# Feed-forward stage of a decoder layer: maxima and projection at other places, weights with semaphores of their own, side taps of the last blocks on ScalarE and GpSimd

## The chip, the cores and the metric

One core of a Trainium2 chip runs the whole layer. The metric is device time in microseconds (us), as the median of the runs of the kernel.

## What is computed

The layer takes x (4 sequences of 1024 tokens, 512 features) and a context, and computes linear attention, then cross attention with an S4D convolution and a feed-forward part, then a convolutional feed-forward with quantised weights and activations; each is followed by a residual and a layer normalisation. Only the last two pieces matter here. Cut to them:

```
h  = layernorm(xt, g_ffn, b_ffn)
xt = xt + gelu(h @ W1 + b1) @ W2 + b2          # 512 -> 2048 -> 512
x2 = layernorm(x1 + layernorm(xt, g_out, b_out))

h = bit_linear(x2, w1)                          # tokens x 2048
h = silu(depthwise_conv1d(h, conv_w, 3 taps) + conv_b)
out = layernorm(x2 + bit_linear(h, w2))
# bit_linear: activations rounded to 8 bits by their row's largest
# absolute value, weights to -1, 0, 1 by their mean absolute value
```

## The kernel before, in words

The change lies in `feed_forward`, the last stage (L1644 on). Each engine has a program of its own, written out by hand in the order in which it runs; semaphores join them. All five programs step through slots `t` = 0 to 38. Slot t does for token tile t (128 tokens, 32 tiles) the products with W1 (`up`, L1868, 16 groups of 128 channels) and with W2 (`down`, L1876). Its layer normalisations are spread over slots t-1 to t+1: `tail_a` to `tail_d` on VectorE (DVE), the square roots (`root`) on ScalarE (ACT), `finish` on GpSimd (POOL). `store_q` writes the rounded tile to memory two slots later.

The convolutional part works on blocks n of 256 tokens, with n = t // 2 - 2. Half of a block's 16 channel tiles is done in an even slot, half in the odd one: `spread` (the product with w1, four matmuls between the groups of `down`, L1887), `dequantise` (DVE, L2117), `centre` (the middle tap, ACT, L1974), `first_tap` and `last_tap` (DVE, L2123 and L2129), `silu` (ACT, L1982). In the next even slot `largest` (DVE, L2159) takes the maxima over the channels, `turn_max` (TensorE, PE, L1895) transposes them, `scales` (DVE) makes the row scales, `spread_scale` (PE, L1900) copies them to all partitions, and `requantise` (DVE, L2179) rounds. In the odd slot after that `project` (PE, L1906, twice 16 matmuls) does the product with w2, `copy_y` (ACT, L1987) empties it, `add_rest` (POOL) adds the residual.

What holds each step, beside its inputs: `up` has 8 places in PSUM and may begin group 8 only when ACT's `gelu` has emptied groups 0 to 3. ACT takes `root(1, t-1)` ahead of `gelu`, and that needs DVE's `tail_a(t-1)`, behind `largest`. The two halves of `project` share one PSUM bank, so the second one waits for `copy_y` of the first. A block's first `spread` waits for the block's inputs, which SP loads (`load_block`, L1800 to L1806) when the last tile of the block's halo has been stored; in three blocks of four that tile is t-2, stored by POOL in the same slot, behind `finish(t-1)`. Blocks 14 and 15 run in slots 32 to 35, in which no tile is left.

At the stage's start SP issues seven small loads, then W1 (4 MB), the next tile and W2 (4 MB); one semaphore, `ff_in`, counts all nine, and every engine waits for all nine.

```
                    if post and not odd:
                        if f == 2:
                            turn_max(n - 1)
                        if f == 9:
                            spread_scale(n - 1)
                    if post and odd and f in (5, 11):
                        project(n - 1, f // 8)
```

Of the kernel before, what the change touches and what calls it, by code (L numbers as in the profile page):

```python
# [1643 lines left out]
def feed_forward(nc, x1, ys, mod_out, W1, b1T, W2, b2, g_ffn, b_ffn, g_out, b_out, eye, x2, q1T, inv_rows,  # L1644
# [6 lines left out]
    with ExitStack() as ctx:  # L1651
# [65 lines left out]
        p_m, p_b = p_mb[:, 0, :].rearrange("p (u n) -> p u n", u=2), p_mb[:, 1, :]  # L1717
        p_y = m.ps("p_y", [P, D])

        (ff_in, consts, h_ready, hT_done, hT_copied, g_done, g_copied, o_done, mod_done, step, pstep, qb_ready, qT_done,  # L1720
         qT_copied, x2_ready, r3_ready, ln_head, out_norm, inv_done) = [m.sem(n) for n in (
             "ff_in consts h_ready hT_done hT_copied g_done g_copied o_done mod_done step pstep qb_ready qT_done "
             "qT_copied x2_ready r3_ready ln_head out_norm inv_done").split()]
        (small_in, tot_ready, sum_done, wm_ready, part_ready, v_ready, c_done, hs_ready, c1_ready, conv_step, c3_ready,
         sl_ready, half_ready, mx_ready, mt_done, dg_ready, b_done, sq_ready, q2_ready, y_done, y_copied, res_ready,
# [34 lines left out]
        def halo(n):  # L1760

            k = n % PB
            return (1 if k == 0 else 0), (WB + 1 if k == PB - 1 else WB + 2)

        block = ctx.enter_context(nc.Block())

        @block.sync
        def _(sp):
# [47 lines left out]
            for n, ap in enumerate((g_ffn, b_ffn, b2, g_out, b_out)):  # L1816
                sp.dma_start(bc[:, n, :], bcast(ap)).then_inc(ff_in, 16)
            sp.dma_start(b1c[:], b1T).then_inc(ff_in, 16)
            sp.dma_start(w1[:], W1.rearrange("(k p) n -> p k n", p=P)).then_inc(ff_in, 16)
            load_tile(1)  # L1820
            load_mod(1)
            sp.dma_start(w2[:], W2.rearrange("(k p) n -> p k n", p=P)).then_inc(ff_in, 16)
            sp.dma_start(cw[:], conv_w).then_inc(small_in, 16)
            sp.dma_start(cb[:], conv_b).then_inc(small_in, 16)
            load_piece(0)
# [19 lines left out]
        def _(pe):  # L1845
# [15 lines left out]

            def up(t, f):
                if f == 0:
                    pe.wait_ge(hT_copied, t + 1)
                if f % 4 == 0:
                    at_least(pe, g_copied, t * FT + f - 4)
                for k in range(KD):
                    last = mm(p_g[:, f % 8, :], w1[:, k, f * P:(f + 1) * P], hT[:, k * P:(k + 1) * P],  # L1868
                              start=(k == 0 and f % 4 == 0), stop=(k == KD - 1 and f % 4 == 3), skip_group_check=True)
                last.then_inc(g_done, 1)  # L1870

            def down(t, f):
                if f == 0:
                    at_least(pe, var[1], t)
                pe.wait_ge(g_copied, t * FT + f + 1)
                last = mm(p_o[:], gT[:, f, :], w2[:, f, :], start=(f == 0), stop=(f == FT - 1))  # L1876
                if f == FT - 1:
                    last.then_inc(o_done, 1)
# [27 lines left out]
                    last = mm(p_y[:], q2[:, f, u * P:(u + 1) * P], v2[:, f, :], start=(f == 0), stop=(f == FT - 1))  # L1906
                last.then_inc(y_done, 1)

            pe.wait_ge(ff_in, 16 * 9)
            pe.wait_ge(consts, 3)  # L1910
            turn_h(0)
            for t in range(SLOTS):
                n, odd = blk(t), t % 2
                ff, bit, post = tile_slot(t), is_blk(n), is_blk(n - 1)
                for f in range(FT):
                    if ff:
                        up(t, f)
                    if f == 3 and tile_slot(t - 2):
                        turn_q(t - 2)
                    if post and not odd:  # L1920
                        if f == 2:
                            turn_max(n - 1)
                        if f == 9:
                            spread_scale(n - 1)
                    if post and odd and f in (5, 11):
                        project(n - 1, f // 8)
                if t == 2:
                    pe.wait_ge(tot_ready, 1)
                    mm(p_b[:, 0:2], ones[:], tot[:], start=True, stop=True).then_inc(sum_done, 1)
                if n == 0 and not odd:  # L1930
                    pe.wait_ge(v_ready, PIECES)
                for f in range(FT):
                    if ff:
                        down(t, f)
                    if bit and not odd and f >= HF:
                        spread(n, f - HF)
                    if bit and odd and f % 2 == 0:
                        spread(n, HF + f // 2)
                    if f == 11 and tile_slot(t + 1):
                        turn_h(t + 1)  # L1940

        @block.scalar
        def _(act):
# [26 lines left out]
            def centre(n, f):  # L1970
                j = n * FT + f
                at_least(act, sl_ready, j - NBUF + 1)
                act.wait_ge(hs_ready, j + 1)
                a(c[:, f % NBUF, :], hs[:, f % NBUF, 1:WB + 1], ACT.Identity, bias=cb[:, f:f + 1],  # L1974
                  scale=cw[:, f, 1:2]).then_inc(c1_ready, 1)

# [11 lines left out]

            act.wait_ge(consts, 3)
            root(0, 0)  # L1990
            act.wait_ge(ff_in, 16 * 9)
            copy_h(0)
            for t in range(SLOTS):
                n, odd = blk(t), t % 2
# [5 lines left out]
                for f in range(FT):  # L2000
                    if ff:
                        gelu(t, f)
                    if f == 7:
                        if post and odd:
                            copy_y(n - 1, 0)
                        if tile_slot(t - 2):
                            copy_q(t - 2)
                    if f == (7 if odd else 11):
                        if tile_slot(t - 1):
                            root(2, t - 1)  # L2010
                        if tile_slot(t + 1):
                            root(0, t + 1)
# [18 lines left out]
        def _(dve):  # L2031
            v = nc.vector
            v.memset(eps[:], LN_EPS).then_inc(consts, 1)
            v.memset(ones[:], 1.0).then_inc(consts, 1)
            dve.wait_ge(ff_in, 16 * 9)
            v.tensor_copy(identb[:], ident[:]).then_inc(consts, 1)
            st = Steps(dve, step, 0)

# [74 lines left out]
            def dequantise(n, f):  # L2113
                j, (lo, hi) = n * FT + f, halo(n)
                at_least(dve, c3_ready, j - NBUF + 1)
                dve.wait_ge(c_done, j + 1)
                v.tensor_tensor(hs[:, f % NBUF, lo:hi], p_c[:, f % 2, lo:hi], rs[:, n % 2, lo:hi], ALU.mult).then_inc(hs_ready, 1)  # L2117

# [13 lines left out]
            def channels(n, half, quarter):  # L2132

                f0 = HF * half
                if quarter == 0:
# [6 lines left out]
                            st.link(v.memset(hs[:, :, WB + 1:WB + 2], 0.0))  # L2142
                    dequantise(n, f0)
                    dequantise(n, f0 + 1)
                for f in range(f0 + HF // 2 * quarter, f0 + HF // 2 * quarter + HF // 2):
                    first_tap(n, f)
                    if f + 2 < f0 + HF:
                        dequantise(n, f + 2)
                    if f > f0:
                        last_tap(n, f - 1)  # L2150
# [50 lines left out]
            for t in range(SLOTS):  # L2201
# [22 lines left out]
                    close_b(n - 2)  # L2224
                if after:
                    head_b(t + 1)
                if before and odd:
                    tail_d(t - 1)
                if t < 2:
                    for i in range(4 * t, 4 * t + 4):  # L2230
# [7 lines left out]
                        quantise(i)  # L2238
                if bit:
                    channels(n, odd, 0)  # L2240
                if before and not odd:
                    tail_d(t - 1)
                if bit:
                    channels(n, odd, 1)
# [3 lines left out]
        @block.gpsimd  # L2248
        def _(pool):
            tt = pool.tensor_tensor  # L2250
            pool.wait_ge(ff_in, 16 * 9)
            st = Steps(pool, pstep, 0)

            def modulate(t):
# [29 lines left out]
            def add_rest(n, u):  # L2284
                pool.wait_ge(y_copied, 2 * n + u + 1)
                pool.wait_ge(b_in[n % 2], 48 * (n // 2 + 1))
                tt(res[:, u, :], res[:, u, :], xb[:, n % 2, u, :], ALU.add).then_inc(res_ready, 1)

            modulate(0)
            affine(0)  # L2290
            for t in range(SLOTS):
# [11 lines left out]
                        add_rest(n - 1, u)  # L2303
                if tile_slot(t - 1):
                    store(t - 1)
            for u in range(4):
                pool.wait_ge(x2_out[u], 16 * (TILES // 4))
                pool.wait_ge(q_out[u], 16 * (TILES // 4))
# [96 lines left out]
```

## Time and profile before

| | us |
|---|---|
| median of 3 runs | 5040.57 |
| lowest, highest | 5039.60, 5043.89 |
| the profiled execution | 5041.77 |
| its span | 5039.7 |
| busy: PE, DVE | 4324.6, 4096.0 |
| busy: ACT, POOL | 2074.3, 2188.5 |

The profile comes from one execution; its span leaves out 2.1 us around it. A timeline row gives the start, the time until the last of the merged instructions has ended, engine, line, operation, what is written and read, and the count; in brackets how long the engine had been idle and what released it. A product of 32-bit numbers is recorded as two matmuls, so a group of `up` is 8 records. The feed-forward stage begins at 3537.8 and takes the last 1502 us.

### The profile page before, as it was taken

The numbers are of one execution on the slowest core, as the hardware profiler recorded it, in microseconds if no ns is written. First come the engines' busy times: TensorE is split into PE (matmuls) and PEld (weight loads), VectorE is DVE, ScalarE is ACT, GpSimd is POOL, SyncE is SP. The second block draws the span as 40 slices with busy tenths as digits, with TensorE's granted clock in tenths as the row PEclk, the third lists the DMA queues.
The fourth block names the chain that finished last, engine by engine and source line by source line (L and its number), as shares of the span: only waits on it lengthen the run. The fifth ranks groups of instructions, "written<-read, shape, count | busy, mean of one in ns | idle before, by whom it ended". The sixth has DMA issues, their size and how long they took to land. (4 is left out here: it accounts for less than half of the span.)

```text
span 5039.7 us, 70649 instructions
## 1 busy us (share of the span) xinstructions
PE 4324.6 (86%) x28037; PEld 3107.2 (62%) x28066; DVE 4096.0 (81%) x4353; ACT 2074.3 (41%) x3688; POOL 2188.5 (43%) x2260
## 2 busy tenths in 40 slices
PE   8999976578889899899899899887578989898984
PEld 6777753256566566566666666667456666666661
DVE  5666659699999999999999999986256767777767
ACT  3433322144444444444444444431234545444453
POOL 1111116434444376677677677660233333333321
PEclk9999988678888788888888888888789999999996
DMA  2111115300001101021101111013531111111101
GB/s 84 51 45 51 49 49 184 120 17 26 31 28 44 45 28 34 30 65 34 32 30 43 57 34 30 28 53 92 194 103 43 61 44 58 47 58 54 51 26 36
DMA packets 214587, 275.98 MB, mean 55 GB/s; under 512 B 96659, under 2 KB 144403, under 8 KB 210224
## 3 DMA queue, kind: packets, MB, share of 16 engines
q1 hardware_dynamic: 196850, 216.91, 14.2%
q0 software_dynamic: 17408, 54.56, 2.9%
q8 instruction: 222, 3.64, 0.3%
q14 instruction: 107, 0.88, 0.1%
HBM read 186.44 MB, written 84.98 MB: 54 GB/s over the span
## 5 line engine op out<-in xcount | busy, mean ns | idle before, releaser
L1548 POOL TENSOR_TENSOR c_s<-c_s,c_z 128x2048 f32<-128x2048 f32 x128 | 581.6, 4544 | 755.6 <-ACT c_z L1333 755.6
L1488 DVE MAX8 c_top<-c_z 128x8 f32<-128x2048 f32 x384 | 878.8, 2288 | 8.8
L1489 DVE MATCH_REPLACE8 c_z<-c_top,c_z 128x2048 f32<-128x2048 f32 x384 | 873.9, 2276 | 0.0
L1174 PEld LDWEIGHTS c_p_a<-c_diag,c_s 128*128 128x128 f32 x4096 | 593.5, 234 | 238.4 <-ACT c_diag L1345 160.6
L1174 PE MATMUL c_p_a<-c_diag,c_s 128*128 128x128 f32 x4096 | 615.8, 321 | 131.3 <-ACT c_diag L1345 95.0
L1164 PE MATMUL c_p_s<-c_kt,c_qT 32*128 32x512 f32 x1024 | 542.4, 920 | 105.1 <-ACT c_s L1327 103.5
L1868 PE MATMUL f_p_g<-f_hT,f_w 128*128 128x128 f32 x4096 | 538.4, 295 | 70.2 <-ACT f_gT L1968 55.7
L1868 PEld LDWEIGHTS f_p_g<-f_hT,f_w 128*128 128x128 f32 x4096 | 526.9, 211 | 90.7 <-ACT f_gT L1968 58.6
L1876 PE MATMUL f_p_o<-f_w,f_gT 128*128 128x512 f32 x1024 | 481.8, 592 | 0.0
L1327 ACT ACTIVATE c_s<-c_p_s 128x512 f32<-128x512 f32 x512 | 286.9, 595 | 362.3 <-PE c_p_s L1165 360.5
L1164 PEld LDWEIGHTS c_p_s<-c_kt,c_qT 32*128 32x128 f32 x1024 | 185.2, 247 | 345.1 <-ACT c_s L1327 321.2
L1226 PE MATMUL c_p_m<-c_aT,c_vals 128*128 128x128 f32 x3072 | 349.8, 276 | 2.5 <-ACT c_aT L1355 2.5
L1244 PE MATMUL c_p_m<-c_wf,c_uT 128*128 128x512 f32 x768 | 350.7, 592 | 0.8 <-ACT c_uT L1360 0.8
L1226 PEld LDWEIGHTS c_p_m<-c_aT,c_vals 128*128 128x128 f32 x3072 | 347.1, 193 | 2.7 <-issue 2.7
L1333 ACT ACTIVATE c_z<-c_z,c_nb 128x2048 f32<-128x2048 f32 x128 | 256.3, 2002 | 213.8 <-DVE c_z L1489 213.7
L1350 ACT ACTIVATE c_s<-c_s,c_nb 128x2048 f32<-128x2048 f32 x128 | 256.0, 2000 | 213.7 <-DVE c_z L1483 213.7
L2117 DVE TENSOR_TENSOR f_hs<-f_p_c,f_rs 128x257 f32<-128x257 f32 (+1 forms) x256 | 108.5, 424 | 231.1 <-PE f_p_c L1887 229.6
L1480 DVE MAX8 c_top<-c_s 128x8 f32<-128x2048 f32 x128 | 292.4, 2284 | 0.0
L1483 DVE MATCH_REPLACE8 c_z<-c_top,c_s 128x2048 f32<-128x2048 f32 x128 | 291.3, 2276 | 0.0
L1876 PEld LDWEIGHTS f_p_o<-f_w,f_gT 128*128 128x128 f32 x1024 | 174.5, 190 | 123.9 <-issue 116.2
L244 PE MATMUL a_p_z<-a_xt,a_w 128*128 128x128 f32 x2048 | 236.1, 276 | 10.9 <-DMA a_w<-in_W_attn 10.9
L244 PEld LDWEIGHTS a_p_z<-a_xt,a_w 128*128 128x128 f32 x2048 | 235.2, 193 | 13.0 <-DMA a_w<-in_W_attn 10.9
(360 smaller groups left out, 7561.4 us busy)
## 6 DMA issues: line engine op xcount, KB each, us to landing
mod_out<-c_fo POOLq DMA_DIRECT2D x32, 512.0 KB, 2.9
f_mr<-mod_out SPq DMA_DIRECT2D x32, 512.0 KB, 4.8
p_ct<-in_ctxT SPq DMA_DIRECT2D x16, 768.0 KB, 4.9
c_vals<-in_ctx SPq DMA_DIRECT2D x4, 3072.0 KB, 12.1
c_kb<-kspec SPq DMA_DIRECT2D x22, 512.0 KB, 4.3
a_xt<-in_xT SPq DMA_DIRECT2D x32, 256.0 KB, 3.1
a_xr<-in_x SPq DMA_DIRECT2D x32, 256.0 KB, 2.6
x<-a_out POOLq DMA_DIRECT2D x32, 256.0 KB, 2.5
```

Of the source, the lines that this page charges most:

```text
L244: last = mm(p_z[:, f, :], w[:, k, f * P:(f + 1) * P], xt[:, t % 2, k, :], start=(f % 4 == 0 and k == 0), stop=(f % 4 == 3 and k == KD - 1) ...
L1164: mm(p_s[:, i, :], qT[r:r + HS, t % 2, :], kt[r:r + HS, cols], start=True, stop=False)
L1174: last = mm(p_a[:, n, :], s[:, h, n * P:(n + 1) * P], diag[:, j % 2, :], start=(h == 0 and n % 4 == 0), stop=(h == NH2 - 1 and n % 4 == 3) ...
L1226: last = mm(p_m[:, 0, k * P:(k + 1) * P], vals[:, n, k * P:(k + 1) * P], aT[:, n, :], start=(k == 0 and n == 0), stop=(k == KV3 - 1 and n ...
L1244: mm(p_m[:, n, :], uT[:, k, :], wf[:, k, c * D:(c + 1) * D], start=(k == 0), stop=False)
L1480: v.max(best[0], s[:, h, :]).then_inc(top1_done, 1)
L1483: v.match_replace(z[:, par, :], best[0], s[:, h, :], NEG).then_inc(s_read, 1)
L1488: st.link(v.max(best[n], z[:, par, :]))
L1489: last = v.match_replace(z[:, par, :], best[n], z[:, par, :], NEG)
L1548: pool.tensor_tensor(s[:, h, :], s[:, h, :], z[:, j % 2, :], ALU.subtract).then_inc(w_ready, 1)
L1868: last = mm(p_g[:, f % 8, :], w1[:, k, f * P:(f + 1) * P], hT[:, k * P:(k + 1) * P], start=(k == 0 and f % 4 == 0), stop=(k == KD - 1 and ...
L1876: last = mm(p_o[:], gT[:, f, :], w2[:, f, :], start=(f == 0), stop=(f == FT - 1))
```

## The change

It has four parts. (1) In even slots `turn_max` stands behind group 9 of `up` and not 2, `spread_scale` behind 15 and not 9; in odd slots `project` stands behind groups 2 and 6 and not 5 and 11, and `copy_y` of the first half behind `gelu` 3 and not 7. (2) W1 and W2 have semaphores of their own, `w1_in` and `w2_in`, awaited by PE ahead of the first group of `up` and of `down`; `ff_in` counts seven loads. (3) In blocks 14 and 15 ACT multiplies both side taps into `side` (which lies over `gT`), and POOL adds them to the middle tap; DVE only dequantises. (4) In slot 32 `tail_d(31)` stands ahead of the block's channels on DVE.

```
+        side = gT[:].rearrange("p (s n a) q -> p s n (a q)", s=2, n=NBUF)
+        def alone(n):
+            return n >= NB - 2
...
-            sp.dma_start(w1[:], W1.rearrange("(k p) n -> p k n", p=P)).then_inc(ff_in, 16)
+            sp.dma_start(w1[:], W1.rearrange("(k p) n -> p k n", p=P)).then_inc(w1_in, 16)
...
-            sp.dma_start(w2[:], W2.rearrange("(k p) n -> p k n", p=P)).then_inc(ff_in, 16)
+            sp.dma_start(w2[:], W2.rearrange("(k p) n -> p k n", p=P)).then_inc(w2_in, 16)
...
             def up(t, f):
                 if f == 0:
+                    pe.wait_ge(w1_in, 16)
                     pe.wait_ge(hT_copied, t + 1)
...
             def down(t, f):
                 if f == 0:
+                    pe.wait_ge(w2_in, 16)
...
-            pe.wait_ge(ff_in, 16 * 9)
+            pe.wait_ge(ff_in, 16 * 7)
...
-                        if f == 2:
+                        if f == 9:
                             turn_max(n - 1)
-                        if f == 9:
+                        if f == 15:
                             spread_scale(n - 1)
-                    if post and odd and f in (5, 11):
-                        project(n - 1, f // 8)
+                    if post and odd and f in (2, 6):
+                        project(n - 1, f // 4)
...
                 act.wait_ge(hs_ready, j + 1)
+                if alone(n):
+                    at_least(act, c3_ready, j - NBUF + 1)
+                    act.wait_ge(o_done, TILES)
+                    for s in range(2):
+                        a(side[:, s, f % NBUF, :], hs[:, f % NBUF, 2 * s:2 * s + WB], ACT.Copy, scale=cw[:, f, 2 * s:2 * s + 1])
...
+                    if f == 3 and post and odd:
+                        copy_y(n - 1, 0)
                     if f == 7:
-                        if post and odd:
-                            copy_y(n - 1, 0)
...
+                if alone(n):
+                    at_least(dve, c1_ready, j - NBUF + 1)
...
+                if alone(n):
+                    for f in range(f0 + 2 + HF // 2 * quarter, min(f0 + 2 + HF // 2 * quarter + HF // 2, f0 + HF)):
+                        dequantise(n, f)
+                    return
...
-                if before and odd:
+                if before and (odd or bit and alone(n)):
                     tail_d(t - 1)
...
+            def taps(n, half):
+                for f in range(HF * half, HF * half + HF):
+                    j, dst = n * FT + f, c[:, f % NBUF, :]
+                    pool.wait_ge(c1_ready, j + 1)
+                    tt(dst, dst, side[:, 0, f % NBUF, :], ALU.add).then_inc(conv_step, 1)
+                    pool.wait_ge(conv_step, j + 1)
+                    tt(dst, dst, side[:, 1, f % NBUF, :], ALU.add).then_inc(c3_ready, 1)
...
+                if is_blk(n) and alone(n):
+                    taps(n, odd)
```

On PE, in an even slot and the odd one after it, the order of `up` (L1868 before, L1875 now) and what stands between its groups (the order counts a group as 4 matmuls). Before, in the even slot:

```order
L1868 MATMUL f_p_g<-f_hT,f_w 128x128 x12
L1895 MATMUL f_p_mb<-f_ident,f_mx 128x128 x2
L1868 MATMUL f_p_g<-f_hT,f_w 128x128 x4
L1859 MATMUL f_p_h<-f_identb,f_qb 128x128 x4
L1868 MATMUL f_p_g<-f_hT,f_w 128x128 x24
L1900 MATMUL f_p_mb<-f_dg,f_ones 128x256
L1868 MATMUL f_p_g<-f_hT,f_w 128x128 x24
```

and now:

```order
L1875 MATMUL f_p_g<-f_hT,f_w 128x128 x16
L1865 MATMUL f_p_h<-f_identb,f_qb 128x128 x4
L1875 MATMUL f_p_g<-f_hT,f_w 128x128 x24
L1903 MATMUL f_p_mb<-f_ident,f_mx 128x128 x2
L1875 MATMUL f_p_g<-f_hT,f_w 128x128 x24
L1908 MATMUL f_p_mb<-f_dg,f_ones 128x256
```

Ten groups stand ahead of the maxima instead of three, and group 8 is now one of them. In the odd slot it is now as follows (before, 24 matmuls stood ahead of the first projection, L1906, and 24 between the two):

```order
L1875 MATMUL f_p_g<-f_hT,f_w 128x128 x12
L1914 MATMUL f_p_y<-f_v,f_q 128x512 x16
L1875 MATMUL f_p_g<-f_hT,f_w 128x128 x4
L1865 MATMUL f_p_h<-f_identb,f_qb 128x128 x4
L1875 MATMUL f_p_g<-f_hT,f_w 128x128 x12
L1914 MATMUL f_p_y<-f_v,f_q 128x512 x16
L1875 MATMUL f_p_g<-f_hT,f_w 128x128 x36
```

Both projections now stand ahead of group 8. On ACT, in the same odd slot, from the last `silu` of the slot before:

```order
L1995 ACTIVATE f_sl<-f_c 128x256 x3
L1956 ACT_TABLE_LOAD
L1956 ACTIVATE f_std<-f_mv,f_eps 128x1
L1976 ACT_TABLE_LOAD
L1976 ACTIVATE f_gT<-f_p_g,f_b1c 128x128 x4
L2000 ACTIVATE f_res<-f_p_y,f_i 128x512
L1976 ACTIVATE f_gT<-f_p_g,f_b1c 128x128 x4
```

The copy of the first projection (L2000, before L1987) has moved ahead of `gelu` 4 to 7, and stays behind the silu, the root and `gelu` 0 to 3.

## Rows read from the trace of the kernel before

**Rows 1.** Windows: slots 28, 29, 9; us, busy PE, PEld, DVE, ACT, POOL, clock, DMA, GB/s
```profile
4739.50:4779.80 40.30, 36.01 (x204) 26.98 (x205) 27.26 (x53) 19.02 (x40) 8.63 (x8) 0.92 0.23 66
4779.80:4824.90 45.10, 41.15 (x233) 28.33 (x233) 33.02 (x59) 22.65 (x48) 20.82 (x19) 0.96 0.09 27
...
3930.70:3974.20 43.50, 39.59 (x232) 26.75 (x232) 33.05 (x59) 22.59 (x48) 20.82 (x19) 1.00 0.19 61
```
**Rows 2.** Timeline of PE, even slot 30
```profile
4832.09 0.69 PE L1895 MATMUL f_p_mb<-f_ident,f_mx 128*128 128x128 f32 x2 [4.27 <-DVE f_mx L2162]
...
4842.05 5.52 PE L1868 MATMUL f_p_g<-f_hT,f_w 128*128 128x128 f32 x48
4847.41 7.89 PE L1876 MATMUL f_p_o<-f_w,f_gT 128*128 128x512 f32 x18
4855.14 0.61 PE L1887 MATMUL f_p_c<-f_qx,f_v 128*128 128x258 bf16 x4
```
**Rows 3.** Timeline of ACT, even slot 30: last root, first four `gelu`
```profile
4833.81 0.28 ACT L1952 ACTIVATE f_std<-f_mv,f_eps 128x2 f32<-128x2 f32 x1
4834.56 1.28 ACT L1968 ACT_TABLE_LOAD   x1 [0.47 <-PE f_p_g L1868]
4835.86 1.15 ACT L1968 ACTIVATE f_gT<-f_p_g,f_b1c 128x128 f32<-128x128 f32 x4
```
**Rows 4.** Timeline of PE, odd slot 29
```profile
4793.66 5.36 PE L1868 MATMUL f_p_g<-f_hT,f_w 128*128 128x128 f32 x32 [2.79 <-ACT f_gT L1968]
4799.07 3.40 PE L1906 MATMUL f_p_y<-f_v,f_q 128*128 128x512 bf16 x15
```
**Rows 5.** Timeline of ACT, odd slot 29: the copy of the first projection
```profile
4794.48 0.74 ACT L1987 ACTIVATE f_res<-f_p_y,f_i 128x512 f32<-128x512 f32 x1
```
**Rows 6.** Timeline of DVE, even slot 30: first step of the scales, first requantise
```profile
4833.49 0.39 DVE L2166 TENSOR_REDUCE f_a<-f_p_mb 128x2 f32<-128x256 f32 x1
...
4842.25 2.29 DVE L2179 TENSOR_TENSOR f_sl<-f_sl,f_p_mb 128x2048 f32<-128x2048 f32 x1 [6.12 <-PE f_p_mb L1900]
```
**Rows 7.** Timeline of POOL, even slot 30: end of `finish`, store of tile 28
```profile
4838.89 1.26 POOL L2271 TENSOR_TENSOR f_r<-f_r,f_xr 128x512 f32<-128x512 f32 x1
4841.96 0.80 POOL L2282 DMA_DIRECT2D q1T<-f_qT  x1 [1.80 <-ACT f_qT L1961]
```
**Rows 8.** Timeline of SP's queue, even slot 30: the block's last load
```profile
4847.25 0.37 SPq L1806 DMA_DIRECT2D f_xb<-x  x1
```
**Rows 9.** DMA issues, that load alone: KB, us to landing
```profile
f_xb<-x SPq DMA_DIRECT2D x1, 512.0 KB, 4.5
```
**Rows 10.** Timeline of SP's queue at the stage's start
```profile
3542.03 1.35 SPq L1818 DMA_DIRECT2D f_b1c<-in_b1T  x1
3543.42 0.94 SPq L1819 DMA_DIRECT2D f_w<-in_W  x1
```
**Rows 11.** DMA issues, the same two, each from a window of its own
```profile
f_b1c<-in_b1T SPq DMA_DIRECT2D x1, 8.0 KB, 7.4
...
f_w<-in_W SPq DMA_DIRECT2D x1, 4096.0 KB, 15.9
```
**Rows 12.** Timeline of POOL: its first instruction of the stage
```profile
3572.89 1.29 POOL L2257 TENSOR_TENSOR f_xt<-f_xt,f_mr 128x512 f32<-128x512 f32 x1 [134.64 <-DMA f_w<-in_W]
```
**Rows 13.** Timeline of DVE, second half of block 14: its first dequantise
```profile
4950.74 0.85 DVE L2117 TENSOR_TENSOR f_hs<-f_p_c,f_rs 128x258 f32<-128x258 f32 x2 [2.04 <-PE f_p_c L1887]
```
**Rows 14.** Timeline of ACT, the same half: its last two `silu`
```profile
4960.37 0.81 ACT L1982 ACTIVATE f_sl<-f_c 128x256 f32<-128x256 f32 x2 [0.64 <-DVE f_c L2129]
```
**Rows 15.** Groups by shape: count, busy us, mean ns, idle before
```profile
L1974 ACT ACTIVATE f_c<-f_hs,f_cb,f_cw 128x256 f32<-128x256 f32 x32 | 18.6, 590 | 27.9 <-DVE f_hs L2117 27.9
...
L832 POOL TENSOR_TENSOR c_fz<-c_fw 128x256 f32<-128x256 f32 x30 | 21.9, 730 | 0.0
```
**Rows 16.** Timeline of DVE, first half of block 14: first and last of `tail_d(31)`
```profile
4936.96 0.16 DVE L2045 RECIPROCAL f_rstd<-f_std 128x1 f32<-128x1 f32 x1
...
4939.62 0.43 DVE L2082 TENSOR_SCALAR f_qb<-f_r 128x512 bf16<-128x512 f32 x1
```

More of the change, by code:

```diff
@@ L1718, in feed_forward @@
         p_y = m.ps("p_y", [P, D])
-        (ff_in, consts, h_ready, hT_done, hT_copied, g_done, g_copied, o_done, mod_done, step, pstep, qb_ready, qT_done,
+        (ff_in, w1_in, w2_in, consts, h_ready, hT_done, hT_copied, g_done, g_copied, o_done, mod_done, step, pstep, qb_ready, qT_done,
          qT_copied, x2_ready, r3_ready, ln_head, out_norm, inv_done) = [m.sem(n) for n in (
-             "ff_in consts h_ready hT_done hT_copied g_done g_copied o_done mod_done step pstep qb_ready qT_done "
+             "ff_in w1_in w2_in consts h_ready hT_done hT_copied g_done g_copied o_done mod_done step pstep qb_ready qT_done "
              "qT_copied x2_ready r3_ready ln_head out_norm inv_done").split()]
@@ L1990, in _ @@
             root(0, 0)
-            act.wait_ge(ff_in, 16 * 9)
+            act.wait_ge(ff_in, 16 * 7)
             copy_h(0)
@@ L2034, in _ @@
             v.memset(ones[:], 1.0).then_inc(consts, 1)
-            dve.wait_ge(ff_in, 16 * 9)
+            dve.wait_ge(ff_in, 16 * 7)
             v.tensor_copy(identb[:], ident[:]).then_inc(consts, 1)
@@ L2240, in _ @@
                     channels(n, odd, 0)
-                if before and not odd:
+                if before and not (odd or bit and alone(n)):
                     tail_d(t - 1)
@@ L2250, in _ @@
             tt = pool.tensor_tensor
-            pool.wait_ge(ff_in, 16 * 9)
+            pool.wait_ge(ff_in, 16 * 7)
             st = Steps(pool, pstep, 0)
```

## The prediction

> **What bounds the kernel now.** I read the table of windows first, then the waits, then PE's and ACT's timelines of one even and one odd slot. The windows [rows 1] show a stage that repeats: an even and an odd slot take 40.3 + 45.1 = 85.4 us, with PE busy for about 90% and every other engine well below. So PE sets the pace, and what counts is where PE stands still. In the even slot that is `turn_max`, 4.27 us behind DVE's maxima [rows 2]; in the odd slot it is group 8 of `up`, 2.79 us, until ACT has emptied groups 0 to 3 [rows 4]. Each standstill costs more than itself: the granted clock of the slots is 0.92 and 0.96 [rows 1], so they hold 2 x 0.08 x 40.3 = 6.4 us and 3.6 us at 1.2 GHz and the rest at 2.4, and PE, busy behind its wait, loses half of them, about 3 and 1.8 us. The chain that ended last can't say more: it follows PE through these slots.
>
> **The even slots (13: t = 6 to 30).** The change takes `turn_max` out of the way, and seven more groups of `up` stand ahead of it. One group costs (4847.41 - 4842.05) / 6 = 0.89 us [rows 2]. But only five of the seven can run. In slot 30 group 2 ended at 4832.09 - 4.27 = 4827.8 [rows 2]; groups 3 to 7 and the tile's transpose end about 4832.5. Group 8 needs `gelu` 0 to 3. ACT is free of its roots at 4833.81 + 0.28 = 4834.1, loads the table (1.28) and takes 1.15 for four `gelu` [rows 3]: 4836.5, whatever PE does, since those roots wait for DVE's `tail_a` behind the same maxima. So PE stands still for 4.0 us at group 8 instead of 4.3 at `turn_max`. Then come eight groups (7.1), `turn_max` (0.7) and `spread_scale` (0.4), and the slow clock's 3 us: `down` starts at 4847.7, against 4847.41. **The wait moves and PE gains nothing.**
>
> What moves with it is late. Behind group 9 at half clock (3.6 us) and its own 0.7 us, `turn_max` ends at 4840.8. `scales` follows it on DVE (before: 4833.49 [rows 6]), and behind `scales`, on the same engine, stands `tail_b`, for which POOL's `finish` waits, and behind that on POOL the store of tile t-2. From `scales` to the end of `finish` it was 4838.89 + 1.26 - 4833.49 = 6.7 us [rows 6, 7], so the store is issued at 4847.5 and not at 4841.96 [rows 7]. From its issue to the landing of the block's last load it was 4847.25 + 4.5 - 4841.96 = 9.8 us [rows 7 to 9], which gives 4857.3; PE wanted that load at 4855.14 [rows 2]. Hence 2.2 us more in the ten even slots whose block needs tile t-2. In the other three only DVE is late: its `requantise` waits for `spread_scale`, which ends near 4847.6 and not 4842.25 [rows 6]; between nothing and those 2.2 us I take 1. Sum: 10 x 2.2 + 3 x 1 = 25 us. Lower end: if the slow stretch is as short as the odd slot's, `turn_max` is 1.4 us earlier, 8 us in all; upper end: the new wait brings a slow stretch of 3.6 us, 10 x 1.8 more, 43.
>
> **The odd slots (13: t = 7 to 31).** Both projections now stand ahead of group 8. The second needs `copy_y` of the first, which stands on ACT behind `gelu` 3 and takes 0.74 us [rows 5]. `gelu` 3 ended when group 8 began, at 4793.66 [rows 4]; so the second projection starts at 4794.4, with 3.3 us of itself [rows 4] and nine groups still to run, 11.3 us, where before 8 groups and a projection, 10.4, remained from 4793.66. That is 0.74 + 0.9 = 1.6 us more. PE gets there one group before it used to reach group 8 (4793.66 - 2.79 = 4790.9), at 4790.0, and stands still for 4.4 us, as long as in the even slot, which had 6.4 us at half clock and not 3.6. With that, 1.4 more is lost. I take the middle, 2.3, since only the clock decides it: 13 x 2.3 = 30 us (21 to 39).
>
> **The stage's start.** POOL's first instruction comes at 3572.89 [rows 12], when W2 has landed. The seven small loads are there at 3542.03 + 7.4 = 3549.4 [rows 10, 11]: 23.5 us earlier. W1 lands at 3543.42 + 15.9 = 3559.3 [rows 10, 11], and `up` of tile 0 follows POOL's first instruction by a dozen microseconds of POOL, DVE and ACT, so it begins near 3561; W2, there at 3572.9, is wanted when its 16 groups of 0.89 us or more have run. Neither is waited for, and what follows (DVE's weight scales) hangs on the same start. **-23.5 us**, between -22 and -24.
>
> **Blocks 14 and 15.** Without tiles, DVE's 1.1 us per channel tile sets the pace: the second half of block 14 takes from 4950.74 to 4960.37 + 0.81 = 4961.2, 10.4 us [rows 13, 14]. Now ACT does three products of 256 columns and a `silu` per tile. The middle tap takes 0.59 alone, about 0.5 back to back; `silu` 0.4 [rows 14, 15]. A side tap, with one pointer operand and not two, lies between those; I take 0.45. Until the last middle tap: 0.5 + 16 x 0.45 + 8 x 0.5 + 5 x 0.4 = 13.7. POOL's two adds then take 0.73 each [rows 15], with `silu` 15.7 in all. So 5.3 us more in each of four halves, and 0.5 more in the two in which the table load is no longer half hidden: 22 us. Against it, `tail_d(31)` leaves the first half, 4939.62 + 0.43 - 4936.96 = 3.1 us less [rows 16], and `close_a` no longer holds up `largest`, at most 1 us twice. **+17 us**; with side taps at 0.4 and 0.5 it is 14 and 20, and 24 if POOL's adds get in DVE's way.
> The Trainium skill, page "ScalarE: Activation LUTs", section "What ACT_TABLE_LOAD costs", gives a fixed part, 0.833 ns per column and about 93 ns for each pointer operand, with as much overlap between neighbours: 0.40 us for a side tap, and a sum 3 us lower than mine.
>
> **The sum.** 25 + 30 - 23.5 + 17 = +48.5 on the profiled execution's 5041.77 us (its span is 5039.7; the rest lies around it): 5090.3, which is 5089 on the scale of the median, 5040.57. The forecast's own ends: 8 + 21 - 24 + 14 = +19, 5060; 43 + 39 - 22 + 24 = +84, 5125.
>
> **Rivals.** (a) The clock stays high. The same wait of the odd slot left slot 9 without any slow stretch: clock 1.00 and 43.5 us instead of 45.1 [rows 1]. If the moved waits fall so in most pairs, an even slot's `turn_max` ends 2 us earlier, the store's load is there in time, and an odd slot comes out where it was: the pairs change by nothing, and the time is 5041 - 23.5 + 17 = 5034. For it: slot 9. Against it: slots 28 and 29, and longer waits than theirs. The Trainium skill, page "TensorE: Matmul & The Clock Gate", section "What's actually happening", says that the activity monitor runs free of the program, so that the same code meets it at another phase; by that rule the even slots' wait could fall either way, and the trace agrees in that slots 9 and 29 differ. (b) **Faster.** The maxima's wait simply goes, with its slow stretch: 4.3 + 3 us in 13 slots, less 1.6 in the odd ones: 13 x 5.7 = 74, so 5041 - 74 - 6.5 = 4960. It decides where `gelu` 3 ends before group 7 does. For it: it is PE's longest wait in the pair. Against: ACT's root ends 6 us behind group 2 [rows 2, 3]. (c) Each of the three waits, the new one at `spread` too, brings its slow stretch and the last halves cost 24 us: about 5123.
>
> **Chances.** The forecast 0.62, (a) 0.12, (b) 0.10, (c) 0.16. A difference under 0.2% (10 us) can't be told from none here. Faster are (b) and a part of (a): 0.12; within 0.2% most of (a): 0.08; slower 0.80. The range leaves (b) out and reaches from (a) to (c): 5033 to 5124.
>
> **What would show it.** PE's waits for `f_mx` near zero, and in their place waits of group 8 for `f_gT` of 4 us in even slots; waits of the second projection for `f_res` of about 4 us in odd slots; waits of `f_p_c` for the load of `f_xb`, 2 us, ten times; first POOL instruction of the stage at 3549.4; four halves of about 16 us at the end, ACT busy throughout. It is wrong if pairs last 85.4 us or less, if group 8 does not wait in even slots, or if the clock in these windows is above 0.96.

## The result, and the profile after

The change makes the kernel slower: 5087.32 us (median of 4 runs, 5079.72 to 5093.79) against 5042.23 (4 runs beside it), ratio 1.0089 with a 95% interval of 1.0071 to 1.0106. The profiled execution took 5088.73 us, its span is 5086.9: 47.2 more than before. The forecast was 48.5 more.

Nothing in the page's shares tells why. The busy times of the changed kernel (engine, us, share, instructions) have hardly moved:

```profile
PE 4331.5 (85%) x28037; PEld 3087.8 (61%) x28066; DVE 4067.6 (80%) x4289; ACT 2095.2 (41%) x3752; POOL 2237.8 (44%) x2324
```

PE is busy for 7 us more, and DVE, the second busiest, for 28 us less. The waits tell it. PE's longest ones between 3780 and 4960 us (the repeating slots, and the beginning of block 14 behind them), first of the kernel before (us in total, times, longest):

```profile
PE f_p_mb L1895 <- DVE f_mx L2162: 62.4, 14, 7.8
PE f_p_g L1868 <- ACT f_gT L1968: 33.4, 12, 2.8
```

and of the changed one:

```profile
PE f_p_y L1914 <- ACT f_res L2000: 57.6, 13, 4.7
PE f_p_g L1875 <- ACT f_gT L1976: 52.8, 13, 4.1
PE f_p_c L1895 <- DMA f_xb<-x: 20.6, 10, 2.7
...
PE f_p_mb L1903 <- DVE f_mx L2181: 7.6, 1, 7.6
```

In the repeating slots, whose last `down` ends at 4904.1 before and 4935.3 now, the maxima were waited for 13 times (54.6 us) and now not at all; one wait for them, of 7.8 and now 7.6 us, lies behind those slots. Group 8 of `up` has taken the place, 4.06 us in each even slot. The odd slot's wait for group 8, 2.79 each, has become one of 4.43 for the copy of the first projection. Ten waits for a block's load are new. The rows before add up to 95.8 us of standstill, those of now to 138.6.

An even slot that follows this through, slot 30, which answers to [rows 2]. PE:

```profile
4854.62 3.81 PE L1875 MATMUL f_p_g<-f_hT,f_w 128*128 128x128 f32 x32 [1.10 <-issue]
...
4866.42 2.89 PE L1875 MATMUL f_p_g<-f_hT,f_w 128*128 128x128 f32 x16 [4.14 <-ACT f_gT L1976]
4869.10 0.63 PE L1903 MATMUL f_p_mb<-f_ident,f_mx 128*128 128x128 f32 x2
...
4875.52 0.60 PE L1908 MATMUL f_p_mb<-f_dg,f_ones 128*128 128x256 f32 x2
4875.95 0.59 PE L1884 MATMUL f_p_o<-f_w,f_gT 128*128 128x512 f32 x1
```

ACT in the same slot, beside [rows 3]:

```profile
4863.44 0.29 ACT L1956 ACTIVATE f_std<-f_mv,f_eps 128x1 f32<-128x1 f32 x1 [5.37 <-DVE f_mv L2054]
...
4863.94 1.28 ACT L1976 ACT_TABLE_LOAD   x1
4865.23 2.17 ACT L1976 ACTIVATE f_gT<-f_p_g,f_b1c 128x128 f32<-128x128 f32 x8
```

and what it waits for on DVE:

```profile
4857.71 3.68 DVE L2178 TENSOR_REDUCE f_mx<-f_sl 128x256 f32<-128x2048 f32 x1
4861.43 0.43 DVE L2181 TENSOR_TENSOR f_mx<-f_mx 128x256 f32<-128x256 f32 x1
4861.77 0.69 DVE L2073 TENSOR_TENSOR f_r<-f_p_o,f_xt 128x512 f32<-128x512 f32 x1
4862.49 0.69 DVE L2053 BATCH_NORM_STATS2 f_stats<-f_r 128x6 f32<-128x512 f32 x1
4863.22 0.18 DVE L2054 BATCH_NORM_AGGREGATE f_mv<-f_stats 128x2 f32<-128x6 f32 x1
```

The reader follows it backwards: group 8 at 4866.42 behind four `gelu`, they behind a table load, that behind the root at 4863.44, that behind DVE's `tail_a` (the last three rows), and that behind the maxima. The maxima still hold PE, 4.1 us and not 4.3, by another name. `down` begins 21.3 us into the slot, where it was 22.5 [rows 2].

What moves with `turn_max` is seen in slot 28, whose block needs tile t-2. POOL's store, beside [rows 7]:

```profile
4788.12 0.80 POOL L2301 DMA_DIRECT2D q1T<-f_qT  x1
```

SP's queue, beside [rows 8]:

```profile
4791.78 0.37 SPq L1812 DMA_DIRECT2D f_xb<-x  x1
```

PE, which had no such wait in [rows 2]:

```profile
4797.28 0.62 PE L1895 MATMUL f_p_c<-f_qx,f_v 128*128 128x257 bf16 x4 [1.96 <-DMA f_xb<-x]
```

The slot begins at 4765.40, so the store is issued 22.7 us into it; before it was 4841.96 - 4824.87 = 17.1. That is 5.6 us later; the prediction had 5.5 (4847.5 and not 4841.96).

PE in odd slot 29, beside [rows 4]:

```profile
4810.23 3.40 PE L1914 MATMUL f_p_y<-f_v,f_q 128*128 128x512 bf16 x15
...
4822.19 5.52 PE L1914 MATMUL f_p_y<-f_v,f_q 128*128 128x512 bf16 x15 [4.71 <-ACT f_res L2000]
```

and ACT, beside [rows 5]:

```profile
4819.94 1.14 ACT L1976 ACTIVATE f_gT<-f_p_g,f_b1c 128x128 f32<-128x128 f32 x4
4820.96 0.70 ACT L2000 ACTIVATE f_res<-f_p_y,f_i 128x512 f32<-128x512 f32 x1
```

The second projection took 3.40 us before [rows 4] and takes 5.52 now, since it comes out of the wait at 1.2 GHz: from 4822 to 4826 the granted clock is 0.50. The windows of slots 28, 29 and 30 (columns as in [rows 1]) show this in the granted clock:

```profile
4765.40:4807.34 41.94, 35.83 (x205) 26.59 (x206) 28.89 (x53) 18.84 (x40) 8.83 (x8) 0.92 0.21 64
4807.34:4854.62 47.28, 41.42 (x233) 27.25 (x233) 31.58 (x59) 22.77 (x48) 20.85 (x19) 0.93 0.09 26
4854.62:4895.06 40.44, 35.27 (x204) 25.84 (x205) 28.74 (x52) 18.72 (x40) 8.88 (x8) 0.96 0.13 40
```

The odd slot is granted 0.93 where it was 0.96 [rows 1].

The wait for the load brings a slow stretch of its own in three of its ten slots, 6, 12 and 22: there `down` is granted 0.92 and takes 21.7 to 22.0 us, in the other seven 1.00 and 18.8 to 20.3. `down` and what follows it in slot 22:

```profile
4517.80:4540.11 22.31, 19.61 (x70) 9.53 (x68) 17.56 (x30) 9.20 (x18) 5.59 (x6) 0.92 0.43 118
```

The table below gives mean lengths in slots 6 to 30 (us; 13 even, 12 odd; the experiments come later). `up` is counted to the start of `down`, and `down` to its own last product. Between that and the next `up` lie 0.3 us in even slots and 1.1 in odd ones, which only the length of the slot has:

| | even: up | down | slot | odd: up | down | slot |
|---|---|---|---|---|---|---|
| before | 22.21 | 17.48 | 39.98 | 25.91 | 17.93 | 44.89 |
| changed | 21.65 | 19.92 | 41.85 | 28.39 | 17.93 | 47.42 |
| e1_start | 22.34 | 17.48 | 40.10 | 26.02 | 17.93 | 45.05 |
| e2_even | 21.94 | 19.53 | 41.76 | 24.87 | 17.93 | 43.85 |
| e3_odd | 22.20 | 17.48 | 39.96 | 27.94 | 17.93 | 46.93 |
| e4_tail | 22.28 | 17.48 | 40.05 | 25.79 | 17.93 | 44.77 |
| e5_tail_a | 15.60 | 20.91 | 36.79 | 28.53 | 17.93 | 47.56 |
| e6_tail_b | 21.81 | 18.85 | 40.94 | 28.56 | 17.93 | 47.59 |
| e9_both | 15.60 | 18.85 | 34.73 | 27.94 | 17.93 | 46.97 |
| e10_dve_order | 23.39 | 17.48 | 41.16 | 25.49 | 17.93 | 44.52 |
| e7_ahead | 16.92 | 17.48 | 34.68 | 25.39 | 17.93 | 44.43 |
| e8_filled | 16.92 | 17.48 | 34.68 | 21.47 | 17.93 | 40.50 |
| e11_spread15 | 15.60 | 18.85 | 34.73 | 21.47 | 17.93 | 40.50 |

At the start POOL comes at 3551.66 (3572.89 before, [rows 12]), behind the small loads:

```profile
3551.66 1.29 POOL L2276 TENSOR_TENSOR f_xt<-f_xt,f_mr 128x512 f32<-128x512 f32 x1 [111.11 <-DMA f_b1c<-in_b1T]
```

At the end, the first half of block 14, from its first dequantise on DVE, then on ACT (its first side taps, a tile in the middle, its last `silu`):

```profile
4961.80 0.43 DVE L2132 TENSOR_TENSOR f_hs<-f_p_c,f_rs 128x258 f32<-128x258 f32 x1 [1.36 <-PE f_p_c L1895]
4962.31 0.91 ACT L1986 ACTIVATE f_gT<-f_hs,f_cw 128x256 f32<-128x256 f32 x2 [9.07 <-DVE f_hs L2132]
4963.12 0.58 ACT L1987 ACTIVATE f_c<-f_hs,f_cb,f_cw 128x256 f32<-128x256 f32 x1
...
4967.92 0.89 ACT L1986 ACTIVATE f_gT<-f_hs,f_cw 128x256 f32<-128x256 f32 x2
...
4969.52 0.89 ACT L1986 ACTIVATE f_gT<-f_hs,f_cw 128x256 f32<-128x256 f32 x2
...
4977.32 0.42 ACT L1995 ACTIVATE f_sl<-f_c 128x256 f32<-128x256 f32 x1 [1.02 <-POOL f_c L2314]
```

and on POOL one tile's first add and the next one's:

```profile
4969.38 0.73 POOL L2312 TENSOR_TENSOR f_c<-f_c,f_gT 128x256 f32<-128x256 f32 x1 [1.08 <-ACT f_c L1987]
...
4970.98 0.73 POOL L2312 TENSOR_TENSOR f_c<-f_c,f_gT 128x256 f32<-128x256 f32 x1
```

A tile takes ACT 1.60 us (4969.52 - 4967.92) and POOL 1.60 (4970.98 - 4969.38), where DVE needed 1.1; from its first dequantise the half lasts until 4977.74, 15.9 us. The same half lasted 14.2 before, with the 3.1 us of `tail_d(31)` in it [rows 16]; its first dequantise and last `silu` before:

```profile
4930.76 0.43 DVE L2117 TENSOR_TENSOR f_hs<-f_p_c,f_rs 128x258 f32<-128x258 f32 x1 [4.41 <-PE f_p_c L1887]
4944.19 0.81 ACT L1982 ACTIVATE f_sl<-f_c 128x256 f32<-128x256 f32 x2 [0.64 <-DVE f_c L2129]
```

The second half of block 14, which answers to [rows 13, 14], lasts 14.5 us where it lasted 10.4:

```profile
4985.12 0.87 DVE L2132 TENSOR_TENSOR f_hs<-f_p_c,f_rs 128x258 f32<-128x258 f32 x2 [3.68 <-PE f_p_c L1895]
4999.23 0.42 ACT L1995 ACTIVATE f_sl<-f_c 128x256 f32<-128x256 f32 x1 [1.03 <-POOL f_c L2314]
```

What the first half has more is a table load of 1.28 us at 4966.31, between its first tiles. Block 15 repeats it: 15.9 and 14.5, where it took 11.2 and 10.4.

**The account of the spans.** `up` of slot 6 starts at 3781.88 (3806.80 before): -24.9. The 25 slots 6 to 30: 13 x 1.87 + 12 x 2.53 = +54.8 (unrounded). Slot 31: +1.2. From the end of its `down` to the end of the span: +16.1. Sum: +47.2. The first term is less sure than the others: in the profiles of nine kernels with the same code up to slot 6 (the change, e1_start, and all that follow e4_tail below), `up` of tile 0 begins anywhere between 3556.9 (e9_both) and 3567.8 (e11_spread15), and slot 6 between 3775.2 and 3788.8.

### The profile page after: what moved, and what is told of

Its sections match the earlier page's. It is cut to its first block and busy times, and to the rows that moved or that the text cites. A ratio compares the mean times of both kernels' runs of the same rounds, so it can differ in the third digit from the quotient of the medians.

```text
span 5086.9 us, 70719 instructions
## 1 busy us (share of the span) xinstructions
PE 4331.5 (85%) x28037; PEld 3087.8 (61%) x28066; DVE 4067.6 (80%) x4289; ACT 2095.2 (41%) x3752; POOL 2237.8 (44%) x2324
## 5 line engine op out<-in xcount | busy, mean ns | idle before, releaser
L1875 PE MATMUL f_p_g<-f_hT,f_w 128*128 128x128 f32 x4096 | 512.3, 287 | 87.5 <-ACT f_gT L1976 72.3
L1875 PEld LDWEIGHTS f_p_g<-f_hT,f_w 128*128 128x128 f32 x4096 | 500.6, 202 | 107.1 <-ACT f_gT L1976 75.4
L2288 POOL TENSOR_TENSOR f_r<-f_r,f_bc 128x512 f32<-128x512 f32 x32 | 40.6, 1268 | 497.2 <-DVE f_r L2060 497.2
## 6 DMA issues: line engine op xcount, KB each, us to landing
c_vals<-in_ctx SPq DMA_DIRECT2D x4, 3072.0 KB, 12.2
```

## The experiments

Four kernels make one part of the change alone.

**e1_start: the weights' own semaphores alone (part 2).**

```
-            sp.dma_start(w1[:], ...).then_inc(ff_in, 16)
+            sp.dma_start(w1[:], ...).then_inc(w1_in, 16)
...
-            pe.wait_ge(ff_in, 16 * 9)
+            pe.wait_ge(ff_in, 16 * 7)
```

> The kernel before with the weights' own semaphores alone (part 2). My theory: the whole stage starts with the small loads instead of with W2, 23.5 us earlier, and nothing later takes it back: 5018, first POOL instruction at 3549. Rival: DVE's weight scales and quantising wait for loads of w1T and w2T that come no earlier, so that the gain is spent by slot 6: 5040 to 5030.

Measured: 5022.55, ratio 0.9962 (0.9947 to 0.9976). 20 us faster. Slot 6 starts 24.3 earlier (3782.54), but the span ends only 20.7 earlier: slots 8 to 11, which took 39.2, 43.5, 39.0 and 43.5 before, take 40.2, 45.0, 40.2 and 45.1. The work in them is the same; slots 9 and 11 were granted 1.00 before and 0.96 here.

**e2_even: `turn_max` behind group 9 and `spread_scale` behind 15 alone.**

```
-                        if f == 2:
+                        if f == 9:
                             turn_max(n - 1)
-                        if f == 9:
+                        if f == 15:
                             spread_scale(n - 1)
```

> The kernel before with the even slots' change alone (turn_max behind group 9, spread_scale behind 15). My theory: the wait moves to group 8 of up, 4 us long, and the late store of tile t-2 makes spread wait about 2 us in ten slots: 25 us slower, 5066, odd slots unchanged at 45.0. Rival (the maxima's wait simply goes): 13 x 7 = 90 us faster, 4950. Rival (the clock stays high): no change, 5041.

Measured: 5058.68 (five runs, 5046.06 to 5061.36), ratio 1.0029 (1.0016 to 1.0043): 16 us slower. The even slots cost what was expected, 13 x 1.8 = 23 us, with the same waits as in the change (group 8 for `f_gT`, ten for the load). But most odd slots came out faster, as slots 16 and 17 show:

```profile
4236.33:4278.27 41.94, 35.96 (x205) 26.72 (x205) 28.93 (x52) 18.87 (x40) 8.82 (x8) 0.92 0.21 64
4278.27:4321.77 43.50, 39.56 (x233) 26.71 (x233) 33.00 (x59) 22.62 (x48) 20.78 (x19) 1.00 0.20 61
```

The odd slot's wait is as long as before, and no stretch at 1.2 GHz follows: 1.00 and 43.50, as in slot 9 of [rows 1]. That is rival (a)'s mechanism, in the odd slots alone, and it gives 12 x 1.04 = 12 us back. Two of the twelve did not gain: slot 19 took 46.4 us and slot 21 44.9.

**e3_odd: both projections ahead of group 8, and the copy at `gelu` 3, alone.**

```
-                    if post and odd and f in (5, 11):
-                        project(n - 1, f // 8)
+                    if post and odd and f in (2, 6):
+                        project(n - 1, f // 4)
...
+                    if f == 3 and post and odd:
+                        copy_y(n - 1, 0)
                     if f == 7:
-                        if post and odd:
-                            copy_y(n - 1, 0)
```

> The kernel before with the odd slots' change alone (project behind groups 2 and 6, copy_y behind gelu 3). My theory: the second projection waits about 4.4 us for copy_y in place of 2.8 at group 8: 1.6 to 3.0 us more per odd slot, 21 to 39 slower, 5070. Rival (clock unchanged, ACT's earlier copy lets groups flow): no change within 5 us. If the even slots cause all of the loss, this run is at 5041.

Measured: 5070.69, ratio 1.0057 (1.0042 to 1.0072): 28 us slower, as expected. The wait for the copy is 57.9 us in 13, where the change has 57.6, and even slots average what they did. In the profile the odd slots account for 12 x 2.04 + 1.2 = 25.7 us; slot 6 began 2.7 later for no reason that lies in this edit.

**e4_tail: side taps on ACT and POOL, `tail_d(31)` ahead (parts 3 and 4) alone.** The edit is those hunks of the diff above.

> The kernel before with blocks 14 and 15 on ScalarE and GpSimd and tail_d(31) earlier (parts 3 and 4) alone. My theory: ACT at 1.8 us per channel tile against DVE's 1.1 sets the pace in four halves: 17 us slower (14 to 24), 5058. Rival: DVE, free of its taps, runs its maxima and roundings beside them, and the tail gets shorter: 5035 or less.

Measured: 5057.02, ratio 1.0028 (1.0016 to 1.0039): 14 us slower, with slots 16 to 30 as before.

The four together make -20.2 + 15.9 + 27.9 + 14.2 = +37.8; the change measured +45.1. The 12 us that e2_even gets back in odd slots are not there once their own wait has been lengthened (clock 0.93); in the profiles slots 6 to 30 cost 38 us in the four together and 55 in the change, against which the starts of slot 6 stand with 8 the other way.

Four more ask for the cause in the even slots. The theory says that DVE's order is at fault, not PE's: `tail_a`, 1.6 us, stands behind the maxima, 4.1 us, and ACT's root needs it.

**e5_tail_a: the changed kernel with `tail_a` ahead of `largest`.**

```
-                if post and not odd:
-                    largest(n - 1, 1)
                 if before:
                     tail_a(t - 1)
+                if post and not odd:
+                    largest(n - 1, 1)
```

> The changed kernel with one thing more: in even slots DVE does tail_a ahead of largest. My theory (group 8 waits in even slots because ACT's root waits for tail_a behind the maxima): gelu 0 to 3 end about 4 us earlier, PE waits neither at group 8 nor at turn_max, its slow stretch goes, and the store of tile t-2 is in time again: even slots from 41.5 to about 34, 5087 - 13 x 7.5 = 4990. Rival: group 8 is held by something else (ACT's own pace, or PE itself): even slots stay within 1 us of 41.5, 5080 to 5090.

Measured: 5027.48, ratio 0.9965 (0.9952 to 0.9978): 60 us faster than the change. The cause is confirmed: group 8 no longer waits in even slots, and `up` lasts 15.6 us, all at full clock. The size fell short of the 4990 expected. Slot 28 shows why, on PE

```profile
4714.18 3.81 PE L1875 MATMUL f_p_g<-f_hT,f_w 128*128 128x128 f32 x32 [1.10 <-issue]
...
4729.80 7.89 PE L1884 MATMUL f_p_o<-f_w,f_gT 128*128 128x512 f32 x18
4740.01 0.62 PE L1895 MATMUL f_p_c<-f_qx,f_v 128*128 128x257 bf16 x4 [2.33 <-DMA f_xb<-x]
```

and on POOL:

```profile
4730.86 0.80 POOL L2301 DMA_DIRECT2D q1T<-f_qT  x1
```

The store is issued 16.7 us into the slot, 6.0 earlier than in the change. But PE reaches the first `spread` 6 us earlier too, and waits as long as ever, 23.6 us in ten, and a slow stretch follows in nine of the ten and not in three: `down` lasts 20.9.

**e6_tail_b: the changed kernel with `tail_b` ahead of `scales`.** Here `finish`, and with it the store, no longer waits for the scales.

```
-                if post and not odd:
-                    scales(n - 1)
                 if before:
                     tail_b(t - 1)
+                if post and not odd:
+                    scales(n - 1)
```

> The changed kernel with tail_b ahead of scales on DVE in even slots, and nothing else. My theory (the late store comes from tail_b standing behind scales, which wait for turn_max): the waits of spread for the load of xb go in slots 6 to 30, down lasts 17.5 us again instead of 19 to 22, 13 x 1.6 = 20 us faster, 5067; the 4 us at group 8 stay. Rival: DVE is as late as the load (its requantise waits for spread_scale), so the wait only changes its name: 5080 to 5087.

Measured: 5081.66, ratio 1.0075 (1.006 to 1.009): 5.7 us less than the change measured, with intervals that overlap. The rival holds. The ten waits for the load are gone from the repeating slots, and `spread` waits for DVE's dequantise instead (7.1 us in 12 waits) and PE's transposes for POOL's `f_h` (5.6 in 12), so that `down` is only 1.07 us shorter, of 2.44 that the change had added. The even slots give 13 x 0.91 = 12 us; 6 of them are lost again in the profile before slot 6, which starts at 3787.71 and not 3781.88, and 2 in the odd slots.

**e9_both: the changed kernel with both swaps.**

> The changed kernel with both swaps on VectorE: in even slots tail_a ahead of largest, and tail_b ahead of scales. With the first swap alone the even slots averaged 36.8 us (up 15.6, down 20.9, of which 2.3 and a slow stretch are the block's late load), 5027. Theory (two causes in series: the root is late by tail_a, and once it is not, the load is late by the store behind finish, which is behind tail_b): both go, the even slot is 15.6 + 17.5 + 0.3 = 33.4 us, 13 x 3.4 = 44 us less than with the first swap: 4983. Rival (as with the second swap alone: the wait for the load goes and one for the first dequantise takes its place, because VectorE is late): down 18.9, 13 x 2 = 26 us less: 5001. In both the odd slots stay at 47.5 us, since nothing there is changed.

Measured: 4996.01, ratio 0.9908 (0.9893 to 0.9924): 91 us faster than the change, and faster than the kernel before. The rival holds again: even slots of 34.7 and not 33.4. The profile comes from the fastest of the four runs, 4983.08 (the others took 4995.77 to 4997.77), and its slot 6 began 6.7 us earlier than the change's. PE's waits for ACT and DVE in its repeating slots (3775.2 to 4830.6):

```profile
PE f_p_y L1914 <- ACT f_res L2000: 57.1, 13, 4.7
...
PE f_p_c L1895 <- DVE f_hs L2132: 6.0, 10, 0.7
```

What is left of the change's cost in the steady slots is the first row, in the odd ones, and 1.37 us of `down` in the even ones, which are shorter than before all the same.

**e10_dve_order: the kernel before with its own semaphores and DVE's two swaps, `turn_max` where it was.**

> The kernel before with the weights' own semaphores and the two swaps on VectorE (tail_a, largest, tail_b, scales), but turn_max at group 2, spread_scale at group 9 and the projections where they were. It asks whether moving turn_max is needed at all. Theory (the move and the order are worth something only together): the wait of turn_max at group 2 is 4.3 us plus the 1.6 us of tail_a now ahead of it, 5.9, with its slow stretch, but the roots no longer wait, so group 8 doesn't; even slots 40.1 + 1.6 = 41.7, less what the earlier store gives (nothing): 5022.6 + 13 x 1.6 = 5043. Rival (the order alone does it): even slots as in the version with turn_max behind group 9, 34.7 us: 4950.

Measured: 5027.92, ratio 0.997 (0.9958 to 0.9981), 5 us above e1_start; the intervals of the two ratios overlap, though no run of the one reaches the other's (5025.55 to 5030.90, and 5021.10 to 5023.09). The order alone gains nothing: PE waits at group 2 for the maxima, 73.6 us in the 13 even slots where e1_start has 54.4. The theory's 5043 was 15 too high: even slots took 1.06 us more than in e1_start and not 1.6, and odd ones 0.53 less.

**e7_ahead: e10_dve_order with `turn_max` at group 9 and `spread_scale` at 12.**

```
-                        if f == 2:
+                        if f == 9:
                             turn_max(n - 1)
-                        if f == 9:
+                        if f == 12:
                             spread_scale(n - 1)
```

> The kernel before with the weights' own semaphores, in even slots DVE in the order tail_a, largest, tail_b, scales, and turn_max behind group 9, spread_scale behind 12; odd slots and the tail as before. My theory: even slots about 34 us instead of 40.3, odd ones 45: 5022 - 13 x 6.3 = 4940. Rival (DVE becomes the bound once PE waits no more): even slots at 37 or above, 4980 or more.

Measured: 4942.66, ratio 0.9799 (0.9783 to 0.9815). Beside e2_even, e10_dve_order and e1_start this settles it. Moving `turn_max` alone costs 16 us (on the kernel before), DVE's order alone about 5 (on e1_start), and the two together gain 80 (on e1_start). e2_even has `spread_scale` at group 15 and this kernel at 12; e11_spread15 below shows that this place makes no difference to the time, there at least. Slots 28 and 29:

```profile
4653.55:4688.32 34.77, 33.59 (x204) 24.42 (x205) 30.50 (x53) 18.95 (x40) 8.81 (x8) 1.00 0.25 77
4688.32:4731.86 43.54, 39.57 (x232) 26.74 (x233) 32.98 (x59) 22.65 (x48) 20.80 (x19) 1.00 0.09 28
```

**e8_filled: e7_ahead with the projections at groups 2 and 7, the first copy moved to ACT's even slot.** The copy stands behind a `silu` there, so PE can fill the odd slot's wait with both projections. What made the change's version wait, the copy behind `gelu` 3, is taken away.

```
-                    if post and odd and f in (5, 11):
-                        project(n - 1, f // 8)
+                    if post and odd and f in (2, 7):
+                        project(n - 1, f // 7)
...
-                        if post and odd:
+                        if post and odd and not bit:
                             copy_y(n - 1, 0)
...
                         silu(n, f)
+                        if post and not odd and f == f0 + 5:
+                            copy_y(n - 1, 0)
```

> The kernel of e7_ahead with the odd slots filled too: project behind groups 2 and 7, and copy_y of the first half in ACT's even slot, behind the silu of channel tile 5, where ACT stood idle. My theory (the second projection waits only because copy_y stands behind gelu 3): the 2.8 us at group 8 are filled by the projection and no wait takes their place, odd slots 40.5 to 42: 13 x 4 us less than e7_ahead, about 4890. Rival (copy_y delays silu and with it the next root and gelu): odd slots 44 or more.

Measured: 4896.15, ratio 0.9707 (0.9693 to 0.9721), against 4890 expected. Slots 28 and 29:

```profile
4614.92:4649.69 34.77, 33.59 (x204) 24.42 (x205) 30.50 (x53) 18.95 (x40) 8.81 (x8) 1.00 0.25 77
4649.69:4690.19 40.50, 39.30 (x232) 26.68 (x233) 31.85 (x59) 22.65 (x48) 20.80 (x19) 1.00 0.10 30
```

Between 3880 and 4760 us PE has no wait above 1.1 us. This version is 2.9% faster than the kernel before.

**e11_spread15: e8_filled with `spread_scale` at group 15.**

> The best version so far (4896: own semaphores, the two swaps on VectorE, turn_max at group 9, spread_scale at 12, projections at groups 2 and 7 with the first copy in the even slot), with spread_scale at group 15 as the change has it. At 12 PE waits there for DVE's f_dg, 21.3 us in 16 waits, 1.1 us or so in each of 13 even slots and a little at half clock: up lasts 17.0 there and 15.6 with spread_scale at 15. Theory: that wait goes, 13 x 1.4 = 18 us less: 4878. Rival: requantise follows spread_scale by three groups later and VectorE, then late, holds the first dequantise of the block, so that down lengthens by as much: 4896.

Measured: 4896.04, ratio 0.9708 (0.9695 to 0.9721): the same. `up` is 1.32 us shorter, `down` 1.37 longer, and the wait has only gone from `f_dg` (12.2 us in 11 even slots) to the dequantise (6.0) and POOL's `f_h` (5.3). DVE is busy for 30.6 of 34.7 us in such a slot; that it now sets the slot's length is likely and was not tried.

## Why the prediction was right

**Even slots, +25:** they cost 24.3 (13 x 1.87). PE stood still 4.06 us at group 8 (4.0 forecast), the ten waits for the load came to 20.6 (22 forecast), and the store was 5.6 us late (5.5 worked out). The sum is nearer than its parts, and that is luck: `up` became 0.56 shorter, where I had 0.3 more, and `down` 2.44 longer, where 25 us in 13, less that 0.3, make 1.6. Over 13 slots the one is 11 us below the forecast and the other 11 above. In the slots that need no load (10, 18 and 26) `down` took 18.89, 1.4 more; I had put 1. In the ten others it took 2.75 more, for 2.06 of wait, and in three of them for the slow stretch that I had left to rival (c). e5, e6 and e9 show both steps to be causes, not companions: take `tail_a` ahead, and group 8's wait goes; take `tail_b` ahead, and the load's, though in e6 alone others take most of its time.

**Odd slots, +30:** 12 x 2.53 + 1.2 in slot 31 = 31.5. The wait was 4.43 (4.4 forecast), and the half clock behind it was what lifted the loss from 1.6 to 2.5: slots 17 and 21, granted 0.96 as before, took 46.7 us, 1.65 more, and the other ten, granted 0.93, 47.2 to 47.9. I had taken 2.3, the middle of its two ends, and which slots get which clock was not foreseen. e3_odd alone gives 25.7 in the same slots.

**Start, -23.5:** `up` of tile 0 began 21.2 earlier in this profile, because SP issued its last small load 2.4 later in the stage's first microseconds (3544.46 against 3542.03, [rows 10]); POOL's start was 3551.66, 7.2 us behind that. By slot 6 it was 24.9. The start scatters by more than this from profile to profile: over the nine with the small loads' start, slot 6 begins at 3784.1 in the mean, over four with the old one (before, e2 to e4) at 3808.6, 24.4 later. The forecast took it that nothing of the head start is lost later; in e1_start 4 us of 24 are given back, in slots granted a lower clock.

**Blocks 14 and 15, +17:** 16.1 in the profile, 14.2 alone. Here too the parts miss and the sum holds. A half without a table load took 14.5 us and not 15.7. A side tap came every 0.405 us back to back ((4963.12 - 4962.31) / 2), not 0.45, which is 0.7 us in a half, and a `silu` 0.3, not 0.4, which is 0.5 in five. The table load in each first half, for which I had put 0.5 more, adds 1.4 (15.9 against 14.5). So the four halves grew by 14.7 us in all, and not by 5.3 x 4 + 1 - 3.1 = 19.1, and the stretches around them by 1.5, where I had 2 less. The Trainium skill, page "ScalarE: Activation LUTs", section "What ACT_TABLE_LOAD costs", led to an estimate of 0.40 for a side tap: the trace agrees with it to 0.005 us. ACT is not alone the bound, since POOL's two adds take the same 1.60 us per tile.

**The rivals.** (b), the wait simply goes, is nearly what the change does with DVE's order changed as well: e9_both has even slots of 34.7 us, where (b) had 40.3 - 7.3 = 33.0, and came at 4996, where (b) had 4960. In the change it is refuted by the 4.06 us at group 8. (a), the clock stays high, did not happen in the change (0.92, 0.93, 0.96 in three slots), but did in e2_even's odd slots and in e7_ahead: the chance of 0.12 was for a real mechanism. (c) is refuted in its size (even slots cost 24 and not 43, the end 16 and not 24), but its mechanism is there: the wait at `spread` brought a slow stretch in three slots of ten, and in e5_tail_a in nine.

The Trainium skill, page "TensorE: Matmul & The Clock Gate", section "What's actually happening", has the activity monitor run free of the program. The runs fit that: with the same 2.8 us wait the odd slot took 43.5, 45.2 or 46.4 us within e7_ahead alone (below). What exactly sets the phase was not tried.

## What to carry to other kernels

When a wait goes, look for the next point on the same engine that hangs on the same producer: here PE's maxima and PE's group 8 both stood behind one 4.1 us stretch of maxima on DVE. The move alone traded one wait for the other, a new order on DVE alone made the wait for the maxima longer, and the two together freed PE of both. An instruction that is taken later on a stalled engine makes everything behind its consumers late, down to a store and a load three engines on; and an engine made faster reaches the next late thing sooner, so that a cure must be worked out against the new time of arrival and not the old.

## What was not expected of the hardware

Identical work with identical waits took different times in odd slots. Slots 13, 15 and 17 of e7_ahead each hold one wait of 2.8 us at group 8, and each follows an even slot of 34.8 us granted 1.00:

```profile
4053.02:4099.43 46.41, 42.44 (x233) 29.63 (x233) 32.92 (x59) 22.66 (x48) 20.77 (x19) 0.93 0.11 38
4134.17:4179.33 45.16, 41.17 (x233) 28.37 (x233) 32.96 (x59) 22.65 (x48) 20.77 (x19) 0.96 0.11 38
4214.08:4257.62 43.54, 39.55 (x233) 26.75 (x233) 32.99 (x59) 22.65 (x48) 20.78 (x19) 1.00 0.20 61
```

So neither the slot itself nor the one before it tells which clock it will be granted. In e2_even this was worth 12 us over the stage, in e1_start 4. A difference of a dozen microseconds between two versions of this kernel can thus come from the granted clock alone. It is out of the way in e8_filled, where no wait in the repeating slots is longer than 1.1 us and all of them are granted 1.00.
